# Expert attention: fc2 bias added ahead of the closing steps, squares for the variance on ScalarE

## What is computed

```
sx   = einsum('bsh,ndh->bnsd', x, hl_w) + hl_b
q, k, v = per expert and head, from sx
out  = causal softmax(q k * 4) v                      # per head and expert
gs   = softmax(out . gate_w + gate_b)                 # over the experts
mixed = sum_e out[e] * gs[e]
hn   = layernorm(mixed + resid)                       # over 16 channels
hx   = relu(hn @ fc1_w.T + fc1_b)
hx   = hx @ fc2_w.T + fc2_b                           # 0 where hn == 0
hx   = layernorm(hx + hn)                             # over 16 channels
fg   = softmax(hx . fgate_w)                          # over the 4 heads
return hx * fg
```

## Time and profile before

| | us |
|---|---|
| three runs | 2023.95, 2024.33, 2016.03 (median 2023.95) |
| profiled execution | 2016.92 |
| its span | 2015.0 |
| PE / PE weight loads busy | 1701.8 / 1243.2 (84% / 62%) |
| DVE busy | 1382.7 (69%) |
| ACT busy | 768.3 (38%) |
| POOL busy | 595.6 (30%) |
| mean granted clock of PE | 0.795 of full |

### The profile page before, as it was taken

How to read it: one execution, slowest core, us unless ns; L and a number is a source line. 1 busy time by engine, 2 the same in 40 slices (tenths; PEclk the granted TensorE clock), 3 DMA queues, 4 the chain that set the end, 5 groups by cost and what they waited for, 6 DMA issues and landing times. The chain is left out here.

```text
span 2015.0 us, 45178 instructions
## 1 busy us (share of the span) xinstructions
PE 1701.8 (84%) x15237; PEld 1243.2 (62%) x15240; DVE 1382.7 (69%) x4295; ACT 768.3 (38%) x2210; POOL 595.6 (30%) x906
## 2 busy tenths in 40 slices
PE   1499999999769899999999999962999999788897
PEld 1266666666535556565555555541888888677776
DVE  6276766666527777777777777774766665688887
ACT  2255444454334444444444444421222222344443
POOL 2522222222134433333333333332211211322221
PEclk9999999999879977777777777765555555687888
DMA  2000000000000000000000000000000000000000
GB/s 114 1 2 0 0 0 0 0 0 0 1 1 2 2 1 0 0 0 0 0 0 0 0 0 0 0 1 0 1 0 0 0 0 1 1 5 6 5 4 13
DMA packets 6978, 8.12 MB, mean 4 GB/s; under 512 B 6272, under 2 KB 6272, under 8 KB 6784
## 3 DMA queue, kind: packets, MB, share of 16 engines
q1 hardware_dynamic: 6912, 7.25, 1.1%
HBM read 5.71 MB, written 1.54 MB: 4 GB/s over the span
## 5 line engine op out<-in xcount | busy, mean ns | idle before, releaser
L604 ACT ACTIVATE al_prob<-al_S,al_negmax 94x94 f32<-94x94 f32 (+1 forms) x512 | 145.9, 376 | 176.2 <-DVE al_negmax L731 176.1
L979 POOL TENSOR_SCALAR_AFFINE_SELECT ex_pT<-ex_pT 128x512 f32<-128x512 f32 (+1 forms) x256 | 129.3, 528 | 246.6 <-ACT ex_pT L1196 195.1
L505 PE MATMUL al_S<-al_kpad,al_qT 128*94 128x376 f32 x384 | 163.0, 507 | 0.0
L1245 DVE TENSOR_REDUCE ex_negmaxA<-ex_R 128x4 bf16<-128x512 f32 x128 | 88.9, 694 | 80.4 <-PE ex_R L1029 78.7
L682 POOL TENSOR_TENSOR al_kpad<-al_kT,al_quad_mask 128x1504 f32<-128x1504 f32 x32 | 86.2, 2694 | 183.7 <-ACTq L619 183.7
L731 DVE TENSOR_REDUCE al_negmax<-al_S 94x2 f32<-94x376 f32 (+1 forms) x192 | 99.2, 542 | 58.4 <-PE al_S L506 52.5
L1595 POOL TENSOR_TENSOR ta_kk<-ta_ext 94x320 f32<-94x320 f32 x64 | 60.4, 962 | 246.2 <-DVE ta_qkn L1775 166.1
L961 POOL TENSOR_TENSOR ex_zrstd<-ex_zvar,neg_half 94x16 f32<-94x16 f32 x34 | 98.6, 2901 | 77.1 <-DVE ex_zvar L1320 77.1
L1170 ACT ACTIVATE ex_pT<-ex_T 128x496 f32<-128x496 f32 x128 | 74.8, 584 | 92.8 <-PE ex_T L1067 92.7
L741 DVE RECIPROCAL al_rec<-al_O 128x188 f32<-128x188 f32 x64 | 84.9, 1327 | 32.1 <-PE al_O L543 32.1
L2004 ACT ACTIVATE mo_hT<-mo_H,wsb 128x188 f32<-128x188 f32 x256 | 88.4, 416 | 38.8 <-PE mo_H L1964 36.2
(11 more groups left out here) (321 smaller groups left out, 4471.2 us busy)
## 6 DMA issues: line engine op xcount, KB each, us to landing
tok_xin<-x_t SPq DMA_DIRECT2D x4, 760.0 KB, 7.2
wsb<-weights SPq DMA_DIRECT2D x1, 2531.0 KB, 13.9
out<-stream SPq DMA_DIRECT2D x16, 94.0 KB
tok_par<-tok_w SPq DMA_DIRECT2D x1, 4.5 KB, 1.6
```

The costliest lines, as they stand in the source:

```text
L505: nc.tensor.matmul(S[0:P, k, 0:2 * N], q, s, start=True, stop=False)
L604: last = nc.scalar.activation(p[:, k, cols], S[0:P, k, cols], ACT.Exp, bias=negmax[g % 2][:, m:m + 1])
L979: nc.gpsimd.affine_select(out=view, in_=view, compare_op=ALU.is_ge, fill=0.0, base=shift, pattern=[[0, NH], [1, cols]], channel_multiplier ...
L1245: red(negmaxA[e % 2][:, D::32], R[:, 0, :].rearrange("p (n s) -> p n s", n=NH), AX.X, ALU.max, negate=True)\
```

## The change

Three things, in the expert attention alone. The addition of fc2's bias on DVE, the last step of a turn, is written ahead of the closing steps of the last stage, behind the gate softmax and mask_values. The square of the centred z, a DVE multiplication into sq, is done by ACT with the function Square, behind its exponentials of e = 1; the subtraction of the mean signals `z_centred` for it, and DVE waits for `sq_ready` before it sums. Two steps fewer are counted on DVE (`STEPS` 23 in place of 25).

```diff
-    STEPS = 25
+    STEPS = 23
...
-                rf, ru, rt, rm, rl = t - FRONT, t - UNIT, t - TAIL, t - MLP, t - LAST
+                rf, ru, rt, rz, rm, rl = t - FRONT, t - UNIT, t - TAIL, t - NORM, t - MLP, t - LAST
...
                         nc.scalar.activation(pT[e % 2][:, 0:2, :], T[:, 0:2, 0:PAIR], ACT.Exp).then_inc(sem["tA_used"], 1)
+                    if e == 1 and valid2(rz):
+                        act.wait_ge(sem["z_centred"], rz + 1)
+                        nc.scalar.activation(sq[:], z[:], ACT.Square).then_inc(sem["sq_ready"], 1)
 
                     if e == 1 and valid(rf):
                         act.wait_ge(sem["kb23_full"], rf + 1)
...
-                    link(tt(groups(z), groups(z), over_components(zmean), ALU.add))
+                    tt(groups(z), groups(z), over_components(zmean), ALU.add).then_inc(sem["z_centred"], 1)
...
                 if valid2(rz):
-                    link(tt(sq[:], z[:], z[:], ALU.mult))
+                    dve.wait_ge(sem["sq_ready"], rz + 1)
                     link(red(zvar[:], groups(sq), AX.X, ALU.add))
...
                 if valid(ru):
                     mask_values(ru, 2, par)
+                if valid(rm):
+                    dve.wait_ge(sem["fc2_full"], rm + 1)
+                    tt(hx[:], X[0:P, 0:HALVES * C].rearrange("p (h c) -> p h c", h=HALVES), over_halves("fc2_b"), ALU.add)\
+                        .then_inc(sem["fc2_used"], 1)
                 if valid(rl):
                     dve.wait_ge(sem["fexp_ready"], rl + 1)
...
                     link(tt(row_halves(rl), row_halves(rl), fout[:], ALU.add))
-                if valid(rm):
-                    dve.wait_ge(sem["fc2_full"], rm + 1)
-                    tt(hx[:], X[0:P, 0:HALVES * C].rearrange("p (h c) -> p h c", h=HALVES), over_halves("fc2_b"), ALU.add)\
-                        .then_inc(sem["fc2_used"], 1)
```

More of the change, by code:

```diff
@@ L859, in expert_attention @@
             fg_used r_full r_used tA_full tA_used tB_full tB_used causal_done o_full o_used gate_ready gexp_ready gs_ready mixed_ready
-            zvar_ready zrstd_ready zn_ready h1m_ready fgate_ready fexp_ready dve_step""".split()
+            z_centred sq_ready zvar_ready zrstd_ready zn_ready h1m_ready fgate_ready fexp_ready dve_step""".split()
         sem = {n: ctx.enter_context(nc.semaphore("ex_" + n)) for n in names}
```

## The result

The changed kernel took **1942.51 us** (median of four runs, 1941.11 to 1943.79) against 2021.39 for the kernel before on the same chip (four runs, 2016.03 to 2024.33): a ratio of **0.961**, 95% interval 0.959 to 0.964. Forecast were 1962 us and a range of 1918 to 2018. Its profiled execution took 1943.79 us, with a span of 1941.8. Of the kernels under Experiments, two with unused matmuls had one execution each that took far longer (2701.29 us of "changed, gap filled", 2389.05 us of "closing steps in slack, gap filled"); no profile shows why, and they are left out of the medians.

A forecast was written before the change was run, and what follows sets the result against it. PE's gaps, and the slow clock behind them, were taken as the bound. 57 us from 25 turns and 5 from the last turns came off 2016.92, giving 1955; 7 more for the median gave 1962 us, range 1918 to 2018.

The forecast's parts named there:

- The gap is not removed but moved: PE's gap of some 1.9 us ahead of zn's transpose goes; one of 2.1 us comes at the first picks.
- The chain to the picks, 7.22 us: From a turn's first scores through bias add, closing steps, DVE's gate steps and ACT's copy to PE's first picks: 7.22 us.
- The two additions at 0.29 us: DVE's additions into z, starting after POOL's mask ended, take 0.29 us each, not 0.73 and 0.47; 0.62 us off.
- The turn at full clock, 20.86 us: 7.22 to the picks plus PE's segments of 1.96, 1.99 and 9.69 make a turn of 20.86 us.
- The clock: PE's clock falls again, now at the picks; turn between 20.86 and 22.73 us, taken as 22.5.
- Rival 1: The clock stays at full: turn 20.86 us, 103 us saved, 1921 us; chance 0.17.
- rival 3: Slower, the clock does not come back within the turn: 28.3 us a turn, 84 us more, 2108 us; chance 0.09.
- rival 2: The slow stretch keeps its length, 11.4 us a turn: turn 24.8 us, only the end's 5 us saved, 2019; chance 0.24.
- faster by more: Chance of being faster by more than the 0.5%, 10 us, that a measurement can tell from no change: given as 0.74.
- The saving of the turns and of the end: 2.28 us in each of 25 turns, 57 us, plus 1 us in five last turns, 5 us.
- The squares: Square moved from DVE to ACT: taken as 0, with 5 us kept for a delayed copy of padded keys.

The follow-up runs named there:

- changed, gap filled: Changed kernel plus six unused matmuls on PE between the sx product and the picks: 1905.76 us, ratio 0.942, turn 20.66 us.
- closing steps in slack, gap filled: Changed kernel with the closing steps behind the first picks, where DVE waited, plus three unused matmuls ahead of the picks: 1888.34 us.
- the move alone: Kernel before with only the bias add moved ahead of the closing steps, square left on DVE: 1944.94 us, ratio 0.963.
- the additions later: Changed kernel with DVE's two additions into z moved from ahead of the maxima to behind mask_values(rt, 3): 1922.73 us, ratio 0.951.

## Why the prediction was right, point by point

**The gap is not removed but moved.** Right. (The 84.3 us of idle time that the prediction starts from is 63.6, as said above; no term of its sum is made of it.) The transpose waits no longer, and the new gap is where it was put, a little shorter: 2.1 us forecast, 0.26 + 1.36 = 1.62 in one turn and 0.46 + 1.42 = 1.88 in the next.

**The chain to the picks, 7.22 us.** Measured 6.77 (901.12 to 907.89), and 7.16 in the next turn (922.58 to 929.74). By its terms in the first: 0.11 to the bias add, as forecast. From the add to the gate maximum 3.49, where the sum had 1.49 + 2.33 = 3.82: the third closing step took 0.37 and not 0.75 us. In both profiles it ends as POOL's product into mixed does (two instructions of 0.64 us each), and now starts in the second of them, before in the first:

```profile
900.93 1.23 POOL L967 TENSOR_TENSOR ex_mixed<-ex_outs,ex_gate 94x256 f32<-94x256 f32 x2 [4.71 <-DVE ex_gate L1365]
```

(POOL, after: the product ends at 902.16, the closing step at 902.19.) Before it was

```profile
920.21 1.23 POOL L967 TENSOR_TENSOR ex_mixed<-ex_outs,ex_gate 94x256 f32<-94x256 f32 x2 [4.10 <-DVE ex_gate L1362]
```

```profile
920.71 0.75 DVE L1370 TENSOR_TENSOR ex_fexp<-ex_fexp,ex_fsum 94x8 f32<-94x8 f32 x1
```

with ends at 921.44 and 921.46. From there to ACT's sxT 2.39, forecast 2.42. ACT to the picks 0.78, forecast 0.87. In every second turn the sum of mixed starts some 0.5 us after the last closing step ends, not 0.1; the program's loop is over two turns, and its jump lies there, which I take for the cause without a run that shows it.

**The two additions at 0.29 us.** Right, 0.29 and 0.28, against 0.61 and 0.47 on average before. POOL's mask ran from 903.97 to 905.06, the first addition began at 905.22. The Trainium skill, GPSIMD Engine Reference, section 1 (Specifications), has POOL and VectorE share SBUF interfaces, with contention for DVE instructions of two SBUF inputs. By that rule, the traces agree: an addition takes 0.28 us alone, and 0.72, 0.76 and 0.47 beside a mask, and the mask itself 1.19 in place of 1.04 where it gives way.

**The turn at full clock, 20.86 us.** The filled kernel shows 20.66, and the one turn of the changed kernel without a slow stretch took 20.93. Counted from its first scores, as in the prediction, that turn has both parts about as forecast: 6.77 us to the picks (858.45 to 865.22), where 7.22 were expected, and 13.77 from there to the next scores (878.99), where 1.96 + 1.99 + 9.69 = 13.64 were.

**The clock.** Right in place, off in size. It fell about at the picks (from 908.8 in one turn, 0.9 us behind them, and from 929.2 in the next, 0.5 us ahead), and came back ahead of the projections of q (at 912.2) or with them (936.1). I had taken 22.5 - 20.86 = 1.64 us for it, near the upper bound of 1.87; it cost 1.44. Rival 1 (no fall) came in one turn of 25, rival 3 (no return) in none, nor did rival 2: the slow stretch did not keep its length when its gap moved. It was above 10 us a turn before and 5 on average after. Why it is shorter no run shows. (Two small slips in the prediction: in rival 3, 28.3 - 24.78 is 3.52 and not 3.6 us a turn, which makes 83 us and not 84, and the chance of "faster by more" adds up to 0.73, not 0.74.)

**The saving of the turns and of the end.** The profiled execution was put at 1955 us and took 1944. The turns gave 66 us, not 57: 0.4 us a turn, half of it in the chain and half in the clock. The end of the stage gave 10.8, forecast 5. I had counted only the wait for the gate product in the last turns; the first turn past the steady ones, with 6.4 us of gain, still had the gap and its slow clock, and was counted in neither term. Against these 15 us stand the 5 by which the stage began later, and 1 of the rest is gained. Then the median: I put it 7 us above the profiled execution, as before; it lies 1 below, another 8 of the 19.5 us that the forecast was too high.

**The squares.** 0 forecast, 0 measured. The duration on ACT is 0.41 us, what DVE needed (0.415). The 0.2 us by which it might delay the copy of padded keys did not show: 0.58 us of idle time lie between them on ACT, and in no steady turn does PE wait for that copy. The Trainium skill, ScalarE: Activation LUTs, section Rules for kernel authors, would give 0.3 us and 0.83 ns an element, as an estimate 0.51 us for 256 elements; the measured 0.41 decides. The same section advises VectorE for products, and here neither engine was the better place, until another edit made the timing matter.

**What I did not see** is the other half of the same reading. The prediction says that the closing steps stand in the chain wherever they are written at the turn's end, and prices 2.33 us of them; and its own timeline showed DVE idle for PE behind the picks. Put there, they cost nothing, and this was worth another 46 us (1942.5 to 1896.9), with the square on ACT.

## What to carry to other kernels

A step that is moved out of one wait's way lands in another's: follow the engine's written order on until the next instruction that another engine waits for, and count the moved gap from there. On TensorE count each recurrent gap twice, as its length and as the granted clock behind it, and test the second with unused matmuls in the gap, a cheap experiment that needs no change of the algorithm. Steps that nobody waits for belong where their engine waits, not at the end of a turn.

## What the runs showed that I had not expected

- The clock fell in 24 of 25 turns behind gaps of 1.35 to 1.46 us in the changed kernel and in 22 of 25 with the move alone, in all 13 behind 1.13 to 1.17 with the additions later, in some turns behind 0.85, 1.07 and 1.09, and in no steady turn of the two kernels with 0.69 and 0.81 as their longest. Which turns it were changed between kernels with nearly the same gaps, in patterns that repeat every two or four turns, so a gap of 1 us or somewhat more has no fixed price. The gap of 1.19 us in the turn from 679 us left the clock at full before; the same gap in the changed kernel's turn from 684 us was followed by 3.4 us at half. In time, 0.24 us on DVE were worth 24 us in one pair of kernels, 0.39 us were worth 7 in another.
- Eight unused matmuls in each turn made the kernel before 2.6% faster.
- A DVE operation on two SBUF inputs that starts while a mask or a product of POOL runs is, in nearly all turns looked at, not slowed in proportion but done when POOL's instruction is, or the next one: the small third closing step within 0.03 us (921.46 against 921.44, and 902.19 against 902.16), the 94x128 ones 0.13 to 0.14 us behind it (before, the product with zn runs from 945.95 to 946.63 and POOL's mask instruction from 945.86 to 946.49). What it costs is set by the moment of its start: 0.75 or 0.37 us for one and the same operation. It is not so beside every POOL instruction: the subtraction of the mean (line 1311) runs beside the small power operation of line 950 and takes 0.42 us, as it does alone. Two additions of 0.28 us each took 0.85 or 1.09 us on DVE, by whether POOL's mask had started 1 to 5 ns ahead of the first of them or 9 to 15; near 5 ns both happened.
